# A recurrent layer: the hidden state turned in two halves, each with a signal of its own

## The reference, cut to what matters

```python
def _lstm(x, W_ih, W_hh, b_ih, b_hh):
    x_proj = jnp.einsum('btd,gd->btg', x, W_ih) + b_ih + b_hh
    def step(carry, xp):
        h, c = carry
        gates = xp + h @ W_hh.T                 # h: 32 x 256, W_hh: 1024 x 256
        i, f, g, o = jnp.split(gates, 4, axis=-1)
        c = jax.nn.sigmoid(f) * c + jax.nn.sigmoid(i) * jnp.tanh(g)
        h = jax.nn.sigmoid(o) * jnp.tanh(c)
        return ((h, c), h)
    _, hs = jax.lax.scan(step, (h0, c0), jnp.swapaxes(x_proj, 0, 1))
```

## Time and profile before

| what | value |
|---|---|
| median of 3 runs | 4548.48 us (4547.19 to 4551.28) |
| profiled execution, its own time | 4549.33 us |
| its span, first to last instruction | 4547.5 us |
| granted TensorE clock, mean | 0.972 |
| busy, share of the span | TensorE 88%, VectorE 76%, ScalarE 63%, GpSimd 26% |
| LSTM steps in the profiled execution | 512, from 3033.3 us to 4470.0 us |

### The profile page before, as it was taken

One profiled execution on the slowest core, in us unless ns is written; L12 is line 12 of the kernel. 1 busy time (PEld: TensorE's weight loads), 2 busy tenths in 40 slices (PEclk: granted clock), 3 DMA queues, 4 the chain that ended last, 5 costly groups with the idle time before them and its releaser, 6 DMA issues. The chain is left out here.

```text
span 4547.5 us, 142915 instructions
## 1 busy us (share of the span) xinstructions
PE 3986.8 (88%) x55570; PEld 2859.9 (63%) x55713; DVE 3476.3 (76%) x9096; ACT 2879.7 (63%) x7042; POOL 1181.9 (26%) x1028
## 2 busy tenths in 40 slices
PE   7999999975999999999997999938888888888882
PEld 5666666642666666666666777727777776777772
DVE  6999999975889888988886888825666666666666
ACT  6999999965888888888884777613333332333330
POOL 4777777760222222222221111000000000000000
PEclk9999999987999999999998999969999999999996
DMA  2222222211000000000003333321121111111115
GB/s 65 70 75 65 67 75 75 75 42 52 29 20 29 29 29 20 29 29 29 23 17 97 133 136 136 106 47 40 34 43 34 43 36 42 36 41 37 40 37 162
DMA packets 326430, 252.61 MB, mean 56 GB/s; under 512 B 171388, under 2 KB 289916, under 8 KB 323708
## 3 DMA queue, kind: packets, MB, share of 16 engines
q1 hardware_dynamic: 324220, 235.03, 17.7%
q10 hardware_dynamic: 1536, 8.39, 0.5%
HBM read 159.43 MB, written 67.11 MB: 50 GB/s over the span
## 5 line engine op out<-in xcount | busy, mean ns | idle before, releaser
L2510 PE MATMUL lstm_G_psum<-lstm_Whh,lstm_HT 128*32 128x192 f32 x8192 | 440.0, 332 | 266.8 <-DVE lstm_HT L2687 266.5
L2580 ACT ACTIVATE lstm_TC<-lstm_G_psum 128x192 f32<-128x192 f32 x512 | 170.5, 333 | 706.7 <-PE lstm_G_psum L2510 706.7
L1534 ACT ACTIVATE ssm_EX<-ssm_Z_psum,ssm_tok 128x256 f32<-128x256 f32 (+1 forms) x1024 | 371.8, 423 | 156.1 <-PE ssm_Z_psum L1364 86.3
L2510 PEld LDWEIGHTS lstm_G_psum<-lstm_Whh,lstm_HT 128*32 128x32 f32 x8192 | 214.2, 109 | 353.8 <-DVE lstm_HT L2687 320.2
L2502 PE MATMUL lstm_G_psum<-lstm_Wih,lstm_XT 128*32 128x192 f32 x8192 | 427.9, 327 | 0.0
L2676 DVE SCALAR_TENSOR_TENSOR lstm_AB<-lstm_TC 128x128 f32<-128x128 f32 x512 | 150.2, 293 | 335.1 <-ACT lstm_TC L2580 331.0
L2840 POOL TENSOR_SCALAR lstm_rstd<-lstm_mv 128x4 f32<-128x4 f32 x32 | 7.2, 225 | 1435.2 <-DVE lstm_mv L2670 1435.2
L541 ACT ACTIVATE g_PR<-g_S,g_nmax 128x512 f32<-128x512 f32 x512 | 367.9, 722 | 1.5 <-DVE g_nmax L676 1.5
L683 DVE COPY g_PT<-g_PT_psum 128x512 f32<-128x512 f32 x512 | 344.3, 683 | 26.1 <-PE g_PT_psum L424 21.4
L532 ACT ACTIVATE g_relu<-g_Z_psum,g_src 128x512 f32<-128x512 f32 x512 | 346.0, 682 | 20.5 <-PE g_Z_psum L417 20.4
L676 DVE CUSTOM_DVE_ANT_0 g_S<-g_Z_psum,g_relu 128x512 f32<-128x512 f32 x512 | 345.5, 684 | 10.2 <-ACT g_relu L532 8.6
(11 more groups left out here) (303 smaller groups left out, 10832.6 us busy)
## 6 DMA issues: line engine op xcount, KB each, us to landing
g_ADJ<-in_adj SPq DMA_DIRECT2D x64, 1024.0 KB, 6.5
x<-g_XO SPq DMA_DIRECT2D x64, 512.0 KB, 5.4
g_X<-in_x SPq DMA_DIRECT2D x32, 512.0 KB, 4.3
ssm_X<-x SPq DMA_DIRECT2D x32, 512.0 KB, 3.9
x<-ssm_OUT SPq DMA_DIRECT2D x32, 512.0 KB, 2.9
g_X<-x SPq DMA_DIRECT2D x32, 512.0 KB, 4.4
lstm_raw<-x SPq DMA_DIRECT2D x1024, 16.0 KB, 1.8
lstm_U<-x SPq DMA_DIRECT2D x128, 128.0 KB, 3.5
```

The lines of the kernel that those rows point to most:

```text
L1534: ins = act.activation(EX[h % NE][:, col:col + n], Zb[c][:, i * CHUNK:i * CHUNK + n], ACT.Exp, bias=tok[b.slot][:, i, c, h:h + 1])
L2510: ins = pe.matmul(bank[32 * j:32 * (j + 1), 0:last - first], HT[t % 2][:, 32 * kc:32 * (kc + 1)], Whh[:, kc, j, first:last], start=False, ...
```

## The change

The transpose at the end of `step` becomes two, one for each half of 32 columns; each adds one to `s["ht"]`. The products of `hidden` wait for the count before each kc, so that those of kc = 0 wait for the first half and those of kc = 1 for the second. All counts of `s["ht"]` are doubled. Nothing else is changed: what is computed, its order and its buffers stay the same.

```diff
             def hidden(c, t):
-                c.wait(pe, s["ht"], S, t + 1)
                 for bank, first, last, made in ((Gb[t % 2], 0, IFG, s["g"]), (Ob[t % 2], IFG, 4 * HB, s["go"])):
                     for kc in range(KC):
+                        c.wait(pe, s["ht"], KC * S, KC * t + kc + 1)
                         for j in range(J):
                             ins = pe.matmul(bank[32 * j:32 * (j + 1), 0:last - first],
...
             def after(c):
-                c.wait(pe, s["ht"], S, S + 1)
+                c.wait(pe, s["ht"], KC * S, KC * (S + 1))
...
-            v.memset(HT[0][:, :], 0.0).then_inc(s["ht"], 1)
+            v.memset(HT[0][:, :], 0.0).then_inc(s["ht"], KC)
             v.wait_ge(s["tot"], 1)
-            v.wait_ge(s["ht"], 1)
+            v.wait_ge(s["ht"], KC)
...
-                v.transpose(HT[(t + 1) % 2][:, :], H[c.slot][:, t, :]).then_inc(s["ht"], 1)
+                for kc in range(KC):
+                    part_of = slice(32 * kc, 32 * (kc + 1))
+                    v.transpose(HT[(t + 1) % 2][:, part_of], H[c.slot][:, t, part_of]).then_inc(s["ht"], 1)
```

## The result

| | before | after |
|---|---|---|
| median of 11 runs | 4547.66 us (4543.75 to 4551.28) | 4535.86 us (4530.57 to 4541.78) |
| ratio | | 0.9974, 95% interval 0.9965 to 0.9984 |
| profiled execution, its own time | 4549.33 us | 4538.08 us |
| first to last H, profiled | 1436.7 us | 1422.6 us |

The change is 11.8 us faster, 7 to 16 by the interval; 4536 was predicted. The profiled execution as a whole gained 11.3 us, since its first H comes 3.2 us later, behind phases whose code is the same.

A forecast was written before the change was run, and what follows sets the result against it. The ring of engines in the 512 recurrent steps was taken as the bound. 31 chunks gaining 0.376 us each (11.7) plus 0.5 for the last gave 12.2 us: 4536, with 8 in 10 between 4518 and 4555.

The forecast's parts named there:

- The ring: TensorE, ScalarE and VectorE wait in turn in the 512 recurrent steps; a step was to fall from 2.80 to 2.76 us.
- First half of the transpose: VectorE's transpose of 32 columns, the only part the ring waits for: 34 ns shorter than the whole's 0.245 us.
- lower end: Lowest bound on the first half's time, from a 128x32 VectorE copy: 0.178 us, a gain of 0.067.
- Second half: VectorE's second transpose: starts 0.136 us after the first, takes 0.211, ends 0.347 after the start of the pair.
- cheaper-halves rival: Transpose's extra goes with its columns: g = 0.067, each half holds VectorE 0.10 us, d = 0.03; 4519 us, chance 0.14.
- TensorE and the late half: Bank G's kc = 1 loads come 0.19 us after the first; second half ready 0.05 before, with 0.16 more slack.
- torn burst: Rival: an unsatisfied wait keeps kc = 1 from loading beside kc = 0's products, bank G 0.16 us later; 4612 us, chance 0.09.
- short restart: Rival: the wait in the middle of TensorE's burst costs 0.024 us again, g = 0.010; 4547 us, chance 0.08.
- Waits on TensorE: Four waits a step ahead of TensorE's products instead of one; a satisfied wait was costed at 0.
- t = 12: Tightest step for VectorE's delayed other work before AB: cover 0.25 us, the change takes 0.13, cost 0.
- The side branch: From t = 7, mv through GpSimd and XN to the tanh of t = 9: 4.18 us instead of 4.08, in 31 chunks.
- g: Gain of a step from the shorter first transpose, 0.034 us; a chunk gains 16g - 2g - d.

The follow-up runs named there:

- halves_one_wait: The change, but TensorE waits for both transposes before its first product: 4579.78 us, ratio to the kernel before 1.0052 to 1.0086.
- between_256: The change, with an extra VectorE addition of 128x256 into an unread tile between the two transposes: 4594.78 us.
- whole_four_waits_by_one: The kernel before, one whole transpose adding 1, with the wait of hidden moved into the kc loop and so asked four times: 4548.25 us.
- after_xn_later: The change, with ScalarE's XN of the next chunk one step later in its queue (t = 9 and 10): 4531.54 us.
- before_xn_later: The kernel before, with ScalarE's XN of the next chunk one step later in its queue (t = 9 and 10): 4546.54 us.
- tc_wait_first: The change, with the wait for tc put ahead of that for to in step: 4518.38 us.
- between_32: The change, with an extra VectorE addition of 128x32 into an unread tile between the two transposes: 4555.87 us.

## Why the prediction was right, point by point

**The ring.** Right. A step fell from 2.80 to 2.76. halves_one_wait shows that this is the early start and nothing else.

**First half of the transpose.** Predicted 0.211 us from the price of a column, measured 211 ns. The lower end of 0.178 is refuted for it.

**Second half.** It starts at its predicted 0.136 (its end at 0.30 less its 0.17). Its own size was wrong: 169 ns, not 211, and the engine is free 0.09 us after its start, not 0.136. A transpose behind a transpose is cheaper: the first half holds the engine for 0.135 us as predicted, the second for about what the cheaper-halves rival gave each (0.10). The mis-sized term is d, the delay of VectorE's other work: 0.06 us, not 0.10.

**TensorE and the late half.** Right: the third four loads keep their 0.19 us. between_256 puts the slack where the prediction had it, 0.16 beyond the load's turn. An unsatisfied wait inside the burst was not in the changed kernel at all, since the second half lands before its turn. In between_256 it is, and the burst loses 0.11 us: 0.08 of delay beyond the slack and 0.024 of restart. The torn burst is refuted: the products of kc = 1 start at 3494.87, while the last of kc = 0, started at 3494.64, takes 0.326 us. The short restart is not refuted: its price shows in between_256, and only its condition, a wait that is not yet satisfied, is missing in the changed kernel.

**Waits on TensorE.** Right, at 0, by whole_four_waits_by_one.

**t = 12.** Cost 0 was right: from H of t = 12 to the next the median of the chunks is 2.76 us, as in the steps around it.

**The side branch.** Right in place, and near in size: 4.15 us instead of the predicted 4.18, XN's wait 22.5/31 = 0.73 instead of 0.78. The traces show it directly, and in after_xn_later the loss is gone from them; the medians of after_xn_later and before_xn_later only lean that way.

**The sum.** With g = 0.034 and the measured d = 0.06 a chunk gains 14 x 0.034 - 0.06 = 0.42 us; 31 of them and 0.5 for the last give 13.4, against 14.1 in the stretch (from the second chunk on, without the first one's wait for its input, 13.0 against 13.4). The forecast of 12.2 was 2 short there. The medians moved by 11.8, which the interval of 7 to 16 does not tell from either, so the closeness of 4536 to 4535.86 is partly luck.

**What it did not see.** In before, H took 256 to 267 ns in 28 of the 31 chunks, always at t = 8 beside GpSimd's `shift`; after, 227 at most. And the changed kernel stands close to the hold-up of GpSimd: its last instruction is spared 0.11 us ahead of the product and held 0.05 ahead of it (tc_wait_first). By between_32 another 0.1 us of VectorE's work turns the gain into a loss. No rival named that.

## What to carry to other kernels

When a result goes round a ring of engines, hand over its first part as soon as the consumer can begin with it: the gain is the latency of the part that is left out, here 34 ns of 245, not half. Then follow the delayed work of the producer to the places where a side branch joins the ring, because they take part of the gain back. Look in the chain for sequencer instructions between two links: the order in which two waits are written is worth 0.07 us a step here, the change 0.04.

## What the runs showed of the hardware

- A 128x32 transpose of VectorE takes 211 ns behind H, for which it waits, 0.20 us behind an addition without a wait, and 169 ns behind a transpose; 128x64 takes 245.
- A wait of TensorE inside a burst of products costs nothing when it is satisfied (4548.25 us beside 4547.39). When it is not, up to 0.16 us behind the loads' turn was covered, and beyond that between_256 paid the delay (0.08) and a restart of 0.024 us.
- In these kernels, of two waits ahead of an instruction, the one written last goes to the sequencer; if it is the late one, the instruction starts 0.10 us after what it waited for instead of 0.035. An instruction that adds 2 to a semaphore sends its wait there too (4579.41 against 4548.25 us).
- A GpSimd instruction on 128x4 elements took 0.71 to 0.77 us instead of 0.23, on the mean of the chunks, when VectorE's 512-column product started 0.01 to 0.05 us behind it; 0.11 us behind it, it took 0.23.
